# Two filler matmuls behind each step of a recurrence, and sixteen in its setup

## The reference, cut to what matters

```
Wx    = batchnorm(x @ W.T, gamma, beta)      # x: 2 batches x 1024 tokens x 32 channels
state = 0
for t in range(1024):
    state = sigmoid(Wx[:, t] + state @ V.T)  # 2 x 32 numbers
    out[:, t] = state
```

## Time and profile before

| | |
|---|---|
| median of 3 runs | 1240.95 us (1239.21 to 1240.99) |
| profiled execution, its own time | 1240.82 us |
| its span, first to last instruction | 1239.0 us |
| mean granted TensorE clock | 0.654 |
| busy share of the span | PE 67%, DVE 39%, ACT 37%, POOL 18% |

### The profile page before, as it was taken

One profiled execution on the slowest core, in us unless ns is written; L12 is line 12 of the kernel. 1 busy time (PEld: TensorE's weight loads), 2 busy tenths in 40 slices (PEclk: granted clock), 3 DMA queues, 4 the chain that ended last, 5 costly groups with the idle time before them and its releaser, 6 DMA issues. The chain is left out here.

```text
span 1239.0 us, 12103 instructions
## 1 busy us (share of the span) xinstructions
PE 835.6 (67%) x4498; PEld 533.5 (43%) x4498; DVE 479.8 (39%) x828; ACT 454.8 (37%) x1547; POOL 226.3 (18%) x130
## 2 busy tenths in 40 slices
PE   3807777777767466455555555588999997547975
PEld 1302323232324223233333333377888886325753
DVE  5588999999656534300000000201000000018652
ACT  3436656565326421233333333322222222335532
POOL 2276666666400000300000000000000000002200
PEclk9957999999975575555555555555555555555985
DMA  2020000000000000100000000000000000000000
GB/s 60 1 51 1 0 1 0 1 1 0 1 4 2 1 19 8 57 0 1 1 1 1 1 1 1 1 1 1 1 1 1 1 1 1 1 1 1 1 20 10
DMA packets 9573, 7.72 MB, mean 6 GB/s; under 512 B 7154, under 2 KB 8066, under 8 KB 9224
## 3 DMA queue, kind: packets, MB, share of 16 engines
q1 hardware_dynamic: 9512, 6.93, 2.4%
HBM read 5.09 MB, written 0.26 MB: 4 GB/s over the span
## 5 line engine op out<-in xcount | busy, mean ns | idle before, releaser
L791 PE MATMUL L2p_z<-L2yx,L2v 64*32 64x2 f32 x2048 | 269.4, 199 | 192.6 <-ACT L2yx L801 186.7
L801 ACT ACTIVATE L2yx<-L2p_z 32x2 f32<-32x2 f32 x1024 | 165.2, 161 | 425.8 <-PE L2p_z L791 425.8
L791 PEld LDWEIGHTS L2p_z<-L2yx,L2v 64*32 64x32 f32 x2048 | 181.7, 136 | 276.4 <-ACT L2yx L801 250.3
L573 POOL TENSOR_TENSOR hc<-hs,cb 128x1024 f32<-128x1024 f32 x64 | 151.1, 2361 | 81.5 <-DVE hs L560 81.5
L560 DVE TENSOR_TENSOR_SCAN hs<-d_a,p_bb 128x1024 f32<-128x1024 f32 x64 | 146.4, 2287 | 9.0 <-ACT d_a L539 0.7
L692 DVE COPY xn<-L2yx 32x512 f32<-32x512 f32 x2 | 0.8, 417 | 332.4 <-ACT L2yx L801 264.1
L526 PE MATMUL p_y<-hc,ident 128*128 128x512 f32 x256 | 122.5, 601 | 3.4 <-POOL hc L573 3.0
L1360 PE MATMUL atp_q<-kk,q 128*128 128x32 f32 x384 | 121.9, 412 | 0.0
L1498 POOL COPY xo<-xn 64x256 f32<-64x256 f32 (+1 forms) x6 | 4.0, 693 | 592.5 <-DVE xn L157 592.5
L539 ACT ACTIVATE d_a<-step,decay 128x1016 f32<-128x1016 f32 x64 | 73.1, 1142 | 87.0 <-DVE hs L560 86.5
L1360 PEld LDWEIGHTS atp_q<-kk,q 128*128 128x128 f32 x384 | 96.1, 310 | 3.0
(11 more groups left out here) (387 smaller groups left out, 918.6 us busy)
## 6 DMA issues: line engine op xcount, KB each, us to landing
y_seq<-in_pick SPq DMA_DIRECT2D x1, 768.0 KB
b_parts<-part SPq DMA_DIRECT2D x3, 256.0 KB, 3.7
c_parts<-part SPq DMA_DIRECT2D x3, 256.0 KB, 4.4
pos<-in_pos SPq DMA_DIRECT2D x1, 512.0 KB, 3.6
ao<-in_at_o SPq DMA_DIRECT2D x1, 512.0 KB, 3.9
L1w<-in_L_w SPq DMA_DIRECT2D x1, 297.0 KB
L3w<-in_L_w SPq DMA_DIRECT2D x1, 297.0 KB
x_tok<-in_x SPq DMA_DIRECT2D x2, 128.0 KB, 2.9
```

Source lines behind the costliest of these rows:

```text
L573: pool.tensor_tensor(hc[:, u % RING], hs[:, u % RING], cb[:, u % RING], ALU.mult).then_inc(sig["hc"], 1)
L791: pe.matmul(p_z[0:C, t % 2, 0:NB], v[:, 0:C], yx[:, NB * t:NB * (t + 1)], start=True, stop=True).then_inc(s("preact"), 1)
L801: act.activation(yx[0:C, NB * (t + 1):NB * (t + 2)], p_z[0:C, t % 2, 0:NB], ACT.Sigmoid).then_inc(s("state"), 1)
```

## The change

In the setup of `L2` POOL makes a bf16 copy of the normalised tokens, `filler` (128 x 512). PE, behind its last useful setup matmul, runs 16 matmuls of 512 columns on it (128 rows, 128 weight columns) into `p_a`, which nobody reads afterwards. In the first recurrent block PE runs such matmuls into bank 1 of `p_z`: five of 512 columns behind step 0, and two of 384 columns behind each of the steps 1 to 516. Their results are never read. The steps' own results all go to bank 0 now, in turn to its two halves. The steps from 517 on and everything else are as before. `L0` takes the old path.

```
@@ recurrent: tiles
+            if not swept:
+                filler = sb(tag + "filler", [128, BANK], BF16, stack=st)
@@ setup, PE
                         if swept:
                             beside.pe_square_sum(pe, p_a)
+                        else:
+                            pe.wait_ge(s("filler"), 1)
+                            for _ in range(16):
+                                pe.matmul(p_a[:, 0:BANK], filler[:, 0:128], filler[:], start=True, stop=True)
@@ setup, POOL
                         pool.memset(yx[0:C, 0:NB * T], 0.0)
+                        if not swept:
+                            norm.wait_tokens(pool)
+                            pool.tensor_copy(filler[:], xn_tok[:].rearrange("p j r -> p (j r)")).then_inc(s("filler"), 1)
@@ first recurrent block, PE
+                    FILL = 384
+                    p_step = p_z[0:C, 0].rearrange("p (h n) -> p h n", h=2)
+                            def fill(n):
+                                pe.matmul(p_z[:, 1, 0:n], filler[:, 0:128], filler[:, 0:n], start=True, stop=True)
                             for t in range(T):
                                 if t:
                                     pe.wait_ge(s("state"), t)
-                                pe.matmul(p_z[0:C, t % 2, 0:NB], v[:, 0:C], yx[:, NB * t:NB * (t + 1)], start=True, stop=True).then_inc(s("preact"), 1)
-                                if t > HALF + 4:
+                                pe.matmul(p_step[:, t % 2, 0:NB], v[:, 0:C], yx[:, NB * t:NB * (t + 1)], start=True, stop=True).then_inc(s("preact"), 1)
+                                if t == 0:
+                                    for _ in range(5):
+                                        fill(BANK)
+                                elif t <= HALF + 4:
+                                    for _ in range(2):
+                                        fill(FILL)
+                                else:
                                     next(others, None)
@@ first recurrent block, ACT
-                                act.activation(yx[0:C, NB * (t + 1):NB * (t + 2)], p_z[0:C, t % 2, 0:NB], ACT.Sigmoid).then_inc(s("state"), 1)
+                                act.activation(yx[0:C, NB * (t + 1):NB * (t + 2)], p_step[:, t % 2, 0:NB], ACT.Sigmoid).then_inc(s("state"), 1)
```

## The result

The changed kernel takes 1276.95 us in the median of 4 runs (1275.78 to 1277.44), the kernel before 1240.08 on the same chip (4 runs, 1239.11 to 1240.99). The ratio is 1.0296, with a 95% interval of 1.0278 to 1.0314: slower by 3%. The forecast was 1275.5 us, the range 1255 to 1312. The span of the profiled execution is 1274.0 us against 1239.0, the mean granted clock 0.769 against 0.654. More of the program runs at 2.4 GHz than before, and it takes longer. The medians are 36.9 us apart and the two profiled executions 35.0; executions of one kernel differ by 2 to 3 us, so what follows goes by the profiled ones.

What follows compares the result with a forecast made beforehand. The latency of alternating matmul and sigmoid was taken to bound the kernel, 0.5125 us a step. 1240.8 + 34.8 (516 longer steps) + 0.5 (setup) - 0.5 (later fast steps) = 1275.6; forecast 1275.5 us, range 1255 to 1312.

Steps and rivals of the forecast that it cites:

- PE's own way: In steps with fillers, PE's path from weight load to next weight load sets the step: 0.58 us at 2.4 GHz.
- the alternation: In the kernel before, PE's matmul pair and ACT's sigmoid strictly wait for each other: 0.5125 us a step.
- (a): From a step's weight load to the first filler's weight load: 0.15 us at 2.4 GHz, bounds 0.10 to 0.20.
- The sum: Over the steps with fillers: 0.0675 us more for each of 516 steps, 34.8 us.
- (b): From the first filler's weight load to the next step's weight load: 0.43 us at 2.4 GHz, bounds 0.40 to 0.48.
- changes of shape: Between 64 x 32 step and 128 x 128 filler weights PE runs empty, twice in each of 516 steps.
- The clock rises in the setup and stays: 2.4 GHz by the end of the setup's sixteen fillers, kept up to step 516, falling soon after.
- the second rival: Clock stays at or falls to 1.2 GHz in the steps: 0.95 us each, 1469 us; half, about 1372; chance 0.10.
- The first rival: Fillers hide between a step's second record and the next weight load: 0.465 us a step, 1216 us; chance 0.09.
- Setup: Ahead of the recurrence, the sixteen fillers delay its start by 0.5 us, at most 1.4.
- the return behind step 516: Some ten steps without fillers still run at 2.4 GHz after the filled ones and give back 0.5 us.
- ACT's idle time: In each step with fillers, ACT idles about 0.42 us.

Runs made afterwards that it cites:

- e3_steps_only: Changed kernel without the setup's sixteen fillers and with only two of 384 columns behind step 0; fillers behind steps 1 to 516 kept: 1465.46 us.
- e1_one512: Changed kernel with one filler of 512 columns instead of two of 384 behind each of steps 1 to 516: 1216.93 us, ratio 0.9822 to the kernel before.
- e7_all384: Changed kernel with one filler of 384 columns behind every one of the 1024 steps instead of two up to 516: 1425.27 us, ratio 1.1501 to the kernel before.
- e1_again: Second measurement of e1_one512, beside e11_longer: 1217.07 us, ratio 0.9817 to the kernel before.
- e5_padded: The control: changed kernel with step tiles zero-padded to 128 rows (weights 128 x 32), fillers still 128 x 128, two of 384 columns: 1280.88 us.
- e9_all512_bridge: Changed kernel with one 512-column filler behind every step, but 14 behind the step where ACT changes its table: 1388.23 us, ratio 1.1205 to the kernel before.
- e4_same_shape: Changed kernel with step tiles zero-padded to 128 rows and the steps' fillers narrowed, so both have 128 x 32 weights: 1223.86 us.
- e8_two256: Changed kernel with two fillers of 256 columns instead of two of 384 behind each of steps 1 to 516: 1221.12 us.
- e10_two320: Changed kernel with two fillers of 320 columns instead of two of 384 behind each of steps 1 to 516: 1248.04 us.
- e11_longer: e1_one512 plus one 512-column filler behind 48 of steps 517 to 572, 14 at ACT's table change: 1226.0 us, ratio 0.9886 to the kernel before.

## Why the prediction was right, by its own steps

- **PE's own way as the bound of a changed step, in place of the alternation: right.** Nearly all of the difference lies in the 516 changed steps, 34.8 of 35.0 us of span. The sum had 34.8. The medians moved by 36.9; the 1.9 between the two is of the size by which executions of one kernel differ.
- **(a), 0.15: right.** 600.31 to 600.46. The row's own value at the lower clock was 0.20, measured there 0.19 (`e3_steps_only`), so the clock gives back the 0.04 to 0.05 that was worked out from the earlier trace rows.
- **(b), 0.43: right.** 600.46 to 600.89. The pair lasts 0.50 as taken from the earlier trace rows, and the filler's first weights are hidden like the others.
- **The cause, changes of shape: right, and now shown.** With one shape the same fillers fit (0.474), with two they don't (0.584, the control). Before the runs against the earlier trace rows were only a correlation. The Trainium skill's "TensorEngine Tiling (Array Packing)" states in "Key Properties" that changing the tiling mode drains TensorE. The control's trace agrees as far as it can: it names the weights' rows and columns, not the mode, and each change of them costs a wait until 0.07 before the modelled end of the matmul ahead.
- **The clock rises in the setup and stays: right.** 1.00 from 512.4 to 819.6 us. `e3_steps_only` shows the second rival at its forecast price, so its 0.10 was for something real: it hung on 21 matmuls ahead of the steps. That wide matmuls in a bit over half of the time would keep the clock was an argument from one stretch, and it was thinner than I wrote: 512 columns behind each step kept it too (`e1_one512`), but 384 lost it (`e7_all384`).
- **The first rival: its mechanism real, its condition not met.** It gave 0.465 a step if the way through PE gets short enough; with 512 columns it is 0.472 and 1216.9 us, where the rival had 1216. I had put the decision into the price of the two shape changes. The columns of the filler decide it as well, and could have been read from the prediction's own terms: 0.15 + 0.39 - 0.07 = 0.47.
- **Small terms.** Setup 0.33 instead of 0.5, but this shows no cost of the setup: in other runs with the same setup the recurrence starts between 513.2 (`e7_all384`) and 515.5 (`e1_again`). For the return behind step 516 I had ten steps and 0.5; eight steps were short (0.472 instead of 0.513), 0.3, and the rest of the layer took 328.7 us against 328.9, 0.2 less. ACT's idle time was forecast at 0.42 and is 0.42. PE's wait no longer being put down to ACT: the brackets still name ACT on PEld, and only the times of the rows show that it was PE.

## What to carry to other kernels

A chain of small dependent matmuls can be made faster by matmuls that nobody reads, if the clock is already up when it starts and stays up, and if the filler's length fits under the other engine's part of the step. Before choosing its length, add up PE's own way, (step's weights to filler's weights) + (filler's length) - (overlap), and compare it with the chain; and give the filler the step's weight shape where that can be done, so that weights can load under a running matmul. Do not let such fillers run on into a stretch where the clock may fall: there each of them costs more than it ever gave.

## What the runs showed of the hardware that I had not expected

- **Whether the clock was up before decides what the same steps get.** Two fillers of 384 columns a step keep it at 2.4 GHz for 300 us if it is up (the changed kernel), and leave it at 1.2 GHz for the whole first half, 488 us, if it isn't (`e3_steps_only`). Two of 320 or of 256 and one of 512 keep it as well; one of 384 did not. These runs do not tell by what measure the chip decides, nor that it raises the clock by another measure than it keeps it: at 1.2 GHz the same step is longer, 0.947 for 0.581, and so holds less filler work in each us.
- **A PE that is shown busy is no sign of it.** PE is at 100% in 600 to 700 us of `e7_all384` and of `e3_steps_only`, at 0.50.
- **A change of rows alone or of columns alone makes the wait.** 128 x 32 to 128 x 128 (`e5_padded`) and 64 x 128 to 128 x 128 (`e9_all512_bridge`) both start 0.07 before the modelled end of the matmul ahead, but 96 and 128 rows with 128 columns go together without it.
- **The stretch behind the layer has two lengths.** From the last sigmoid to the end it takes 129.8 to 130.3 us in seven of the profiled executions (the kernels before and after, `e3_steps_only`, `e4_same_shape`, `e8_two256`, `e10_two320`, `e11_longer`) and 127.7 to 128.5 in the other seven, with the same instructions in it. The windows of `e8_two256` and of `e1_one512` in the attention:

```profile
1160.00:1170.00 10.00, 9.40 (x55) 7.10 (x56) 5.67 (x28) 5.27 (x17) 0.00 (x0) 0.83 0.00 0
```

```profile
1160.00:1170.00 10.00, 10.00 (x83) 8.10 (x82) 5.05 (x25) 4.60 (x16) 0.00 (x0) 1.00 0.00 0
```

In `e8_two256`, as in the other six of the longer kind, the clock dips in the attention for 3.4 us; in none of the seven shorter ones does it. What sets this off was not tried and stays open, also whether it goes with the kernel or changes from one execution to the next. It means that 2.5 us of any two profiles' difference here may come from a stage that neither kernel touches: the profiled span of `e1_one512` is 24.2 us shorter than that of the kernel before, 21.2 of them in the steps and 2.5 in this stretch.
